# A transformer block with cross-attention and experts: score and maxima matmuls on the two halves of the array

## The reference, cut to what matters

```
q, k, v = heads(x @ Wq + bq), heads(x @ Wk + bk), heads(x @ Wv + bv)
y  = softmax(where(causal, q k^T * scale, -inf)) @ v
qc, kc, vc = heads(x @ Wcq + bcq), heads(ctx @ Wck + bck), heads(ctx @ Wcv + bcv)
y += softmax(qc kc^T * scale) @ vc
x  = x + tanh(g_xattn) * (y @ Wp + bp)
x  = x + tanh(g_ffn) * (top-4 of 32 experts and a shared one, of layernorm(x))
```

## Time and profile before

| | us |
|---|---|
| median of three runs | 4757.66 |
| lowest and highest | 4754.53, 4763.01 |
| the profiled execution: span (first to last instruction) | 4808.0 |
| PE busy | 4323.8 (90%) |
| DVE busy | 3532.5 (73%) |
| ACT busy | 2688.0 (56%) |
| POOL busy | 1651.4 (34%) |
| maxima matmuls of the context, line 570 | 971.4 in 3072 |
| score matmuls, line 492 | 1291.0 in 4352 |
| their reductions on DVE, line 882, context | 1999.1 in 3328 |

### The profile page before, as it was taken

How to read it: one execution, slowest core, us unless ns; L and a number is a source line. 1 busy time by engine, 2 the same in 40 slices (tenths; PEclk the granted TensorE clock), 3 DMA queues, 4 the chain that set the end, 5 groups by cost and what they waited for, 6 DMA issues and landing times. The chain is left out here.

```text
span 4808.0 us, 75133 instructions
## 1 busy us (share of the span) xinstructions
PE 4323.8 (90%) x25317; PEld 1906.7 (40%) x25317; DVE 3532.5 (73%) x7733; ACT 2688.0 (56%) x5523; POOL 1651.4 (34%) x2163
## 2 busy tenths in 40 slices
PE   5999999999999999999999999999999995688882
PEld 2333333334343433333333333333333332577771
DVE  5788788888878787878788878788888783344443
ACT  1665656565656565665656565656665653344440
POOL 1122323232323232323232232323232314488883
PEclk7999999999999999999999999999999997899996
DMA  5443545454444344545444545454544444888888
GB/s 118 71 91 75 109 84 106 81 111 81 106 81 104 73 104 84 110 84 108 86 104 87 102 82 107 80 104 90 100 94 99 95 97 131 184 150 150 151 150 245
DMA packets 363501, 513.23 MB, mean 107 GB/s; under 512 B 64124, under 2 KB 227820, under 8 KB 363176
## 3 DMA queue, kind: packets, MB, share of 16 engines
q1 hardware_dynamic: 268240, 380.43, 38.0%
q0 software_dynamic: 87728, 115.39, 13.6%
q10 hardware_dynamic: 7208, 13.26, 0.9%
HBM read 288.49 MB, written 201.27 MB: 102 GB/s over the span
## 5 line engine op out<-in xcount | busy, mean ns | idle before, releaser
L688 ACT ACTIVATE prob<-scores 128x512 f32<-128x512 f32 (+3 forms) x4352 | 2141.6, 561 | 1268.5 <-PE scores L492 1251.6
L882 DVE TENSOR_REDUCE pmx<-ring 128x1 f32<-128x512 f32 (+1 forms) x3328 | 1999.1, 664 | 165.1 <-PE ring L570 158.3
L492 PE MATMUL scores<-stacks 98*128 98x512 bf16 (+3 forms) x4352 | 1291.0, 370 | 79.5 <-ACT prob L688 31.0
L514 PE MATMUL outs<-prob,vt 128*32 128x512 f32 x8704 | 1094.3, 575 | 4.9 <-POOL prob L1084 3.9
L570 PE MATMUL ring<-stacks 96*128 96x512 bf16 x3072 | 971.4, 389 | 64.1 <-DVE pmx L882 55.6
L492 PEld LDWEIGHTS scores<-stacks 98*128 98x128 bf16 (+1 forms) x4352 | 341.0, 99 | 1299.4 <-ACT prob L688 736.3
L1598 POOL DMA_INDIRECT scratch_sums<-e_yo,e_tok x320 | 496.3, 1551 | 116.7 <-issue 84.1
L882 DVE TENSOR_REDUCE mc<-ring 128x1 f32<-128x128 f32 (+3 forms) x1024 | 437.3, 483 | 123.1 <-PE ring L587 119.0
L1084 POOL TENSOR_SCALAR_AFFINE_SELECT prob<-prob 128x512 f32<-128x512 f32 x256 | 168.4, 658 | 1045.9 <-ACT prob L688 1036.0
L1154 POOL TENSOR_TENSOR split<-rest,split 128x512 bf16<-128x512 f32 (+1 forms) x224 | 218.8, 977 | 803.5 <-DVE split L976 803.0
L570 PEld LDWEIGHTS ring<-stacks 96*128 96x128 bf16 x3072 | 301.2, 99 | 450.9 <-DVE pmx L882 184.6
(11 more groups left out here) (165 smaller groups left out, 3751.4 us busy)
## 6 DMA issues: line engine op xcount, KB each, us to landing
stacks<-scratch_parts SPq DMA_DIRECT2D x768, 128.0 KB, 7.2
stacks<-scratch_parts SPq DMA_DIRECT2D x384, 136.1 KB, 10.0
scratch_parts<-split SPq DMA_DIRECT2D x64, 768.0 KB, 4.5
e_xin<-scratch_slots SPq DMA_DIRECT2D x160, 289.0 KB
scratch_parts<-split SPq DMA_DIRECT2D x32, 816.8 KB, 4.5
num<-oc POOLq DMA_DIRECT2D x256, 64.0 KB
den<-scratch_inverses POOLq DMA_DIRECT2D x63, 256.0 KB, 8.4
ct<-in_ctx_t_dram SPq DMA_DIRECT2D x16, 800.5 KB, 8.1
```

Source lines behind the costliest of these rows:

```text
L492: eng.matmul(ps[0:m, k, q0:T], kst[g][0:KR + 2, j, k0:k0 + m], qst[g][0:KR + 2, j, qc + q0:qc + T], start=True, stop=True).then_inc(scored ...
L514: mm = eng.matmul(po[32 * j:32 * j + 32, q0:T], vt[ch][0:m, VW * vi + VE * hl:VW * vi + VE * hl + 32], prob[0:m, n % 2, j, q0:T], start=kt ...
L688: eng.activation(prob[0:m, n % 2, j, q0:T], ps[0:m, i % SB, q0:T], ACT.Exp, scale=SCALE).then_inc(exped.sem, 1)
L882: eng.tensor_reduce(dst, src, AX.X, ALU.max).then_inc(free_of(part, it), 1)
```

## The change

The stack of a head is cut into two steps (`STEPS`): 64 rows with the first four products of pieces, and 34 rows with the last two and the shift rows. Even heads of a pair lie on partitions 0 to 63, odd ones on 64 to 127, so that a matmul uses a 64x128 tile of the array, upper or lower. A head's scores are two accumulating matmuls instead of one. A pair's are issued in the order first step even, first step odd, second step even, second step odd. Maxima use the first step alone, one matmul per head, the two heads of a pair behind each other in two ring banks; the mask of `own` becomes two 64-row steps for each head. The stack loads are twice as many and half as large, the shift rows go out in four DMAs instead of two.

In the plan an item of maxima now stands for a pair of heads. The table `MAXIMA` is gone, and `M` uses the even dealing of `F` and `L`. Work that needs the whole array (`WHOLE_ARRAY`) stands in odd places only, after the maxima, directly before the weighted sum.

```diff
-LOADS, CONSTS = 9 + 2 + 4 + 3 + 2, 14
+LOADS, CONSTS = 9 + 2 + 4 + 3 + 2, 19
 def max_items(g):
-    out = [("own", g, j, qt) for j in range(4) for qt in range(NQ)]
-    costs = [0.35 + 0.18 * qt for j in range(4) for qt in range(NQ)]
-    for j in range(4):
-        out += [("cross", g, j, qt, part) for qt in range(NQ) for part in range(3)] + [("rest", g, j)]
-        costs += [0.82] * (3 * NQ) + [0.46]
+    out = [("own", g, pair, qt) for pair in range(2) for qt in range(NQ)]
+    costs = [0.7 + 0.3 * qt for pair in range(2) for qt in range(NQ)]
+    for pair in range(2):
+        out += [("cross", g, pair, qt, part) for qt in range(NQ) for part in range(3)] + [("rest", g, pair)]
+        costs += [1.2] * (3 * NQ) + [0.8]
...
-DEFERRED = ("split", "value", "shift", "outproj", "hidden", "shared")
-MAXIMA = {
-    0: (5, 4, 1, 1, 4, 0, 1, 3, 2, 1, 3, 2, 4, 2, 2, 3, 2, 3, 2, 3, 2, 3, 3, 3, 3, 2, 2, 2),
...
+WHOLE_ARRAY = ("trans", "split", "value", "shift", "outproj", "router", "hidden", "shared", "rank")
...
-        if kind == "M":
-            for n, k in zip(range(lo, hi), MAXIMA[lo]):
...
-        deal(0, (57, 60, 63, 66, 69, 72, 75), split_items(0), 1.8)
-        deal(HALF, range(24, 41, 4), value_items(0), 1.35)
-        deal(HALF, range(47, 66, 3), split_items(1), 1.8)
+        deal(0, (57, 61, 63, 67, 69, 73, 75), split_items(0), 1.8)
+        deal(HALF, range(25, 42, 4), value_items(0), 1.35)
+        deal(HALF, (47, 51, 53, 57, 59, 63, 65), split_items(1), 1.8)
...
-BANKS = {"trans": 1, "split": 1, "value": 1, "own": 1, "cross": 1, "rest": 1, "shift": 1, "outproj": 1, "router": 1,
+BANKS = {"trans": 1, "split": 1, "value": 1, "own": 2, "cross": 2, "rest": 2, "shift": 1, "outproj": 1, "router": 1,
...
-    KR = D * len(QP)
+    STEPS = ((0, 4), (4, 6))
+    PR = D * STEPS[0][1]
+    SR = D * (STEPS[1][1] - STEPS[1][0])
...
-                for p in range(2):
-                    j, i = 2 * pair + p, 4 * n + 2 * pair + p
-                    k = i % SB
-                    before = i - SB if i >= SB else max(j for j in range(4 * SLOTS) if j % SB == k) - 4 * SLOTS
-                    pe.wait_ge(exped, part, before + 1)
-                    pe.wait_ge(rowed[g], part, row_no(g))
-                    eng.matmul(ps[0:m, k, q0:T], kst[g][0:KR + 2, j, k0:k0 + m],
-                               qst[g][0:KR + 2, j, qc + q0:qc + T], start=True, stop=True).then_inc(scored.sem, 1)
+                for step in range(2):
+                    for side in range(2):
+                        i = 4 * n + 2 * pair + side
+                        k = i % SB
+                        before = i - SB if i >= SB else max(j for j in range(4 * SLOTS) if j % SB == k) - 4 * SLOTS
+                        pe.wait_ge(exped, part, before + 1)
+                        pe.wait_ge(rowed[g], part, row_no(g))
+                        on = slice(64 * side, 64 * side + (SR + 2 if step else PR))
+                        mm = eng.matmul(ps[0:m, k, q0:T], kst[g][step][on, pair, k0:k0 + m],
+                                        qst[g][step][on, pair, qc + q0:qc + T], start=step == 0, stop=step == 1)
+                        if step:
+                            mm.then_inc(scored.sem, 1)
...
-                    dst = take(part, it)
                     pe.wait_ge(stacked_rest[g], part, load_no(part, g))
-                    eng.matmul(dst, qst[g][0:KR, j, 128 * qt:128 * qt + 128],
-                               kst[g][0:KR, j, T + 512 * of:T + 512 * of + 512], start=True, stop=True).then_inc(ring.sem, 1)
+                    for side in range(2):
+                        dst = take(part, it, side)
+                        on = slice(64 * side, 64 * side + PR)
+                        eng.matmul(dst, qst[g][0][on, pair, 128 * qt:128 * qt + 128],
+                                   kst[g][0][on, pair, T + 512 * of:T + 512 * of + 512], start=True, stop=True).then_inc(ring.sem, 1)
...
-                    for r, src in enumerate(parts):
-                        eng.dma_start(dst[g][D * r:D * r + D, :, c0:c0 + cn],
-                                      scr["parts"][ch, PIECES.index(kind), src][64 * v:64 * v + 64, 0:cn].rearrange(
-                                          "(h d) c -> d h c", d=D)).then_inc(done[g].sem, 16)
+                    for step, (lo, hi) in enumerate(STEPS):
+                        for r in range(lo, hi):
+                            src = scr["parts"][ch, PIECES.index(kind), parts[r]][64 * v:64 * v + 64, 0:cn].rearrange(
+                                "(p s d) c -> s d p c", p=2, s=2)
+                            for side in range(2):
+                                at = 64 * side + D * (r - lo)
+                                eng.dma_start(dst[g][step][at:at + D, :, c0:c0 + cn], src[side]).then_inc(done[g].sem, 16)
...
                     for i in range(2):
-                        eng.dma_start(qst[g][KR + i:KR + i + 1, :, :].rearrange("o t c -> o (t c)"), mr[:, i, :]
-                                      ).then_inc(rowed[g].sem, 16)
+                        for side in range(2):
+                            at = 64 * side + SR + i
+                            eng.dma_start(qst[g][1][at:at + 1, :, :].rearrange("o t c -> o (t c)"), mr[16 * side:16 * side + 16, i, :]
+                                          ).then_inc(rowed[g].sem, 16)
```

More of the change, by code:

```diff
@@ L572, in item @@
                 elif what == "rest":
-                    g, j = it[1:]
-                    dst = take(part, it)
+                    g, pair = it[1:]
                     pe.wait_ge(stacked_rest[g], part, load_no(part, g))
+                    dsts = [take(part, it, side) for side in range(2)]
                     for qt in range(NQ):
-                        mm = eng.matmul(dst[:, 66 * qt:66 * qt + 66], qst[g][0:KR, j, 128 * qt:128 * qt + 128],
-                                        kst[g][0:KR, j, T + TC - 66:T + TC], start=True, stop=True)
-                        if qt == NQ - 1:
-                            mm.then_inc(ring.sem, 1)
+                        for side in range(2):
+                            on = slice(64 * side, 64 * side + PR)
+                            mm = eng.matmul(dsts[side][:, 66 * qt:66 * qt + 66], qst[g][0][on, pair, 128 * qt:128 * qt + 128],
+                                            kst[g][0][on, pair, T + TC - 66:T + TC], start=True, stop=True)
+                            if qt == NQ - 1:
+                                mm.then_inc(ring.sem, 1)
@@ L581, in item @@
                 elif what == "own":
-                    g, j, qt = it[1:]
+                    g, pair, qt = it[1:]
                     n = 128 * (qt + 1)
-                    dst = take(part, it)
                     pe.wait_ge(stacked[g], part, load_no(part, g))
-                    eng.matmul(dst[:, 0:n], qst[g][0:KR, j, T + 128 * qt:T + n], kst[g][0:KR, j, 0:n], start=True, stop=False)
-                    eng.matmul(dst[:, 128 * qt:n], identb[:, :], maskb[:, :], start=False, stop=True).then_inc(ring.sem, 1)
+                    dsts = [take(part, it, side) for side in range(2)]
@@ new lines, in item @@
+                    for side in range(2):
+                        on = slice(64 * side, 64 * side + PR)
+                        eng.matmul(dsts[side][:, 0:n], qst[g][0][on, pair, T + 128 * qt:T + n], kst[g][0][on, pair, 0:n],
+                                   start=True, stop=False)
+                    for half in range(2):
+                        for side in range(2):
+                            on = slice(64 * side, 64 * side + 64)
+                            mm = eng.matmul(dsts[side][:, n - 128 + 64 * half:n], identb[on, 64 - 64 * half:192 - 64 * half], maskb[on, 0:128 - 64 * half],
+                                            start=False, stop=half == 1)
+                            if half:
+                                mm.then_inc(ring.sem, 1)
@@ L885, in item @@
                     for last in max_items(g)[0][-RB:]:
-                        read(dve, part, last)
+                        for side in range(2):
+                            read(dve, part, last, side)
                     eng.tensor_reduce(mc[g % 2][:, :].rearrange("p (h a q) -> p h a q", a=2, q=NQ)[:, :, 0, :], pmx[:, :, :, :],
```

87 lines of the change are left out of this document (47 added, 40 removed), and 3 rows, old and new, of the table MAXIMA.

## The result

The changed kernel takes **5114.89 us** (median of 4 runs, 5105.74 to 5118.78) where the kernel before took 4760.34 beside it (4 runs, 4754.53 to 4766.18): a ratio of **1.0741, 95% interval 1.0726 to 1.0757**, 354 us slower. The forecast was slower, at 4873 us with a range of its own up to 5000: the sign is right, the size (+115) a third of what came.

The account below looks back on a forecast made before the run. The prediction took a PE, ACT, PE chain per slot plus stalls around DVE as the bound. Middle batches +98, first +9 and last +8 sum to +115 on 4757.7, giving 4873 us, own range 4740 to 5000.

Parts of the forecast that it names:

- What bounds the kernel: Middle batch: a PE, ACT, PE chain sets a slot's least time; arithmetic 224 us, plus 23 us of stalls around DVE.
- Scores, +26: Bare slots: the even head completes after two widths, so a slot grows from 2.40 to 2.82 us, +26 us a batch.
- Maxima and cover: Slot places: 26 us of maxima columns leave a batch; first-place excess vanishes, -22 us; second places go 49 to 53, +4.
- shape change: 35 second places of a batch have one more array shape change at 0.12 us: +4 us, bounds 0 and 8.
- The order of the work: Middle batches: replacing the hand-made table of maxima by the first batch's rule costs nothing, up to 5 us.
- Stalls, 17 of 23: Stalls around DVE in a middle batch: 17 of the 23 us stay, bounds 8 and 23.
- First and last batch: First batch: arithmetic 222 and 16 us of stall, +9; last batch: +15 of arithmetic, stall 30 to 22, +8.
- The 50 us carried over: Whole kernel: the profiled span lies 50 us over the median of 4757.66, and this difference is carried over to the forecast.
- 1: Middle batches: the longer chain hides as well, DVE stalls fall to the lower bound, about 4700 us; chance 0.14.
- 2: Slots: PE's columns decide, so the saved columns come back whole, -22 us in 14 batches, about 4415 us; chance 0.08.
- 3: Half-array matmuls: the halves don't run side by side, a batch gets 40 to 50 us longer, 5400 to 5550; chance 0.07.
- 4: Weight loads of a half wait for that half's matmul, about +0.25 us a slot, +17 a batch, about 5130; chance 0.06.

Follow-up runs that it names:

- cheap maxima: Each kernel with DVE's full maxima read over 256 of 512 columns, PE's work unchanged: changed kernel 5016.24 us, kernel before 4700.09 us.
- run with one step: Changed kernel with scores only from the second step of 34 rows, the first 64 rows left out: 5042.03 us, ratio 1.058.

## Why the prediction was wrong, and where it was right

**What bounds the kernel: right for most slots.** The slot arithmetic carried over. 39 of the 68 slots of a middle batch take the same time, within 0.03 us at full clock, with full and with cheap maxima, as a chain of PE and ACT should: 3.04 us with one pair of maxima in each place (2.82 + 0.21), and 4.74 for the slot from 2185.14, with its four projection passes (2.82 + 1.71 + 0.20). The twenty that are longer are DVE's.

**Scores, +26: right in the bare slot,** which took 2.83 for 2.82. The run with one step bears the size out in part: 11.7 us a batch in the 59 slots that could be read at full clock.

**Maxima and cover, -26 of columns, -22 of excess, +4 in second places: right within the chain.** The chain went from 224 to 240 in place of 237; the 3 us are the **shape change, sized at 0.12 and measured at 0.20** (7 us for 4, inside the bounds of 0 to 8). The Trainium skill (TensorEngine Tiling (Array Packing), Key Properties) says that a change of mode drains the engine; the trace agrees as far as each change costs 0.11 us. One sign failed: the maxima's busy time was to halve, and fell from 971 to 765 us, because each record holds the matmul's way through the array as well as its columns.

**The order of the work, "at nothing, up to 5" for the kernel: the step that failed first.** The forecast priced only the loss of the hand-made table, and not the new places nor the dealing in twos. In timed runs the three are 60, 14 and 50 us. At full clock they are 1.2, 0.2 and 3.4 us a batch, 67 us in M; where the rest of the 124 us is the profiles do not say, since before's was taken at a time when its set stood higher.

**Stalls, 17 of 23: right in what the halves take off, wrong in what they are taken from.** The time over the chain is 19 us at full clock before (243.2 less 224), 25 in the kernel that has the change's order with whole-array matmuls (248.0 less 223), and 19 in the changed one (258.8 less 240); by the lines of the last section 21, 27 and 23. So longer slots and more cover did take 4 to 6 us off, as the forecast reckoned, but the order had put 6 on. The picture behind the 23 was too simple as well: nearly 4 of them were clock (52 us in fourteen batches), and of the other 19 the maxima being late is 5 before and 9 after, by the slots that shrink with cheap maxima. Which waits the rest is was not separated.

**The clock: not in the forecast at all.** 101 us are counted as lost in M instead of 52, at most 3.5 us a batch more, and 1 by the lines. It fell 42 times in the changed kernel's fourteen middle batches and 24 times before. One of these falls, in windows of the changed kernel:

```profile
2135.19:2143.19 8.00, 5.32 (x46) 1.64 (x49) 7.73 (x19) 4.28 (x8) 0.00 (x0) 0.99 0.55 160
2143.19:2147.19 4.00, 4.00 (x24) 0.81 (x20) 2.52 (x7) 1.56 (x3) 0.00 (x0) 0.59 0.00 0
```

Eight microseconds with PE busy 5.32, then 4 at 0.59 of the clock. The change makes PE wait longer in each slot (0.47 for ACT where it was 0.26) and halves the maxima that filled it. That this is why the clock falls more often is argued, not shown, and two rows of the table speak against it as the whole reason.

**The sum for a middle batch** is then: forecast 254, measured 266; 3 of the 12 us are the chain, about 6 the order, 1 to 3.5 the clock. In fourteen batches that is 168 us of the miss.

**First and last batch: +9 and +8 became +20 and +19,** as if each were a middle batch. They were not taken apart; in the last the mean granted clock is 0.93 where it was 0.97. Two slips of the sum are small beside this: +15 less 8 is +7 for the last batch, not +8, and 254 less 246.6 is 7.4, which makes 104 in fourteen batches and not 98.

**The 50 us carried over: wrong.** +115 became +306 between the profiled spans, 191 us, and 50 us more because the changed kernel's profile is at its median (5113.9 and 5114.89) while before's is not. That is the miss of 242. What puts the kernel before at 4760 in one set of runs and at 4808 to 4820 in another is not known; it is not the granted clock, which is alike in both. So 48 of the 354 us are in no profile.

**Rivals.** 1 and 2 asked for a batch of 245 or less, and it was 266. 3 and 4 are refuted in the bare slot, though 4's 5130 us is nearly the time that came: that is luck, and a time near a rival's is no evidence for its mechanism. The Trainium skill (TensorE: Matmul & The Clock Gate, The mechanism) has loads overlap only when the row group differs; the trace does not bear it out: the kernel before loaded 98-row weights under running 98-row matmuls (three loads in 0.33 under three matmuls in 0.82), and the changed kernel's period of 2.83 is the chain with no load in it. **Stack loads at nothing: right**; they land sooner than before, 2.8 and 2.6 us from issue by the page, and no score waits for them. The sign "PE idle before scores, tens of us a batch" is 13 in one middle batch, from 5.

## To carry to other kernels

Halving TensorE's columns in a stage where it waits on a chain of engines buys little, and a pass added to the chain is paid in every slot. Before pricing such an edit, count how many slots end on the chain, how many passes stand on it, and where the trace already shows the clock at its lower level. Order found by trial (a table, places, the depth of a ring) is a term with a price, not a detail: here 124 us for the order and over 300 for one bank of four. Build the new order with the old instructions first, since that splits the two in one run. And a stall beside a busy engine should be tested by making that engine's work cheaper, and read slot by slot, since the gain of some slots can come back as a wait in others.

## What the runs showed of the hardware that I had not expected

- Two matmuls of 64 rows in the two halves take one width (0.44 us for four of 512 columns), but a change between this shape and the whole array costs 0.11 us each way. 64-row maxima without a partner made the kernel take 1.0948 times as long, a part of it by a lower clock.
- The granted clock falls to 1.2 GHz in a kernel that looks fully busy: 10 us at a time and more, up to 24 in the one-step kernel. There 59 of 68 slots became 11.7 us a batch shorter and the other nine, most of them at a low clock, 7.9 longer.
- The same program's median moved from 4760 to 4816 us between sets of runs, 1.2%, with the granted clock the same (0.961 and 0.960 on the mean). A profiled span has to be compared with its own set's times.
